# Gate logits and the turn of x1 into user-major rows: two TensorE products against one of 136 columns

## The chip, the cores and the metric

The kernel runs on one core of one Trainium2 chip. The metric is the device time of one execution in microseconds (us). The kernel before has been run three times: the median is 1422.55 us (1422.31 to 1427.97).

## What is computed

The reference is a graph layer followed by a mixture of eight experts, for 10000 users of 128 features. Cut to what matters:

```python
h = item_feat @ W_item.T + b_item
x1 = x + relu(adj @ h + layernorm(x) @ W_user.T + b_user)      # adj is 10000 x 10000, float32
t = layernorm(x1)
logits = t @ gate_w + gate_b                                   # eight experts
idx = argmax(softmax(logits)); prb = the largest probability
pos = the user's place among those of its expert; kept = pos < 1563
y = relu(t @ w1[idx] + b1[idx]) @ w2[idx] + b2[idx]            # 128 -> 512 -> 128
out = x1 + nan_to_num(y * prb * kept)
```

## The kernel before, in words

**Work and stages.** The users are cut into 20 blocks of 500 (four tiles of 125, `TILES`, `TP`). For each block the product with the 400 MB matrix `adj` runs over the 10000 items in 20 groups `g` of four chunks of 128 items (the last group has three). Each number of `adj` and of `h` is split into a high and a low part, and three products (high x high, high x low, low x high) of 500 columns each go into one PSUM bank, `acc[q]`, with `q` the block's parity. The result is feature-major: features on partitions, users along the columns.

**Who does what in a group.** SyncE (SP, L372) loads the group into a ring of ten buffers; ScalarE (ACT, L483) makes the high part into a ring of four; VectorE (DVE, L672) makes the low part; TensorE (PE) does eight products from the high part (L1077, L1079) and, one group later, four from the low part (L1088). Semaphores `hi_used` and `lo_used` give the buffers back.

**What follows a block.** The order is written out by hand in the `body` of each engine. In block `b` each engine, between two groups, also does a piece of the blocks `b-1` and `b-2`:
- ACT takes the accumulator of block `b-1` through relu into `gnn` (`take_gnn`, L493, group 4); DVE adds x to it (`add_x`, L709, group 5). `gnn` is then x1, feature-major.
- PE, behind the low part in group 5, runs `logits(b-1)` (L1120): four products with a tile of `gnn` as the stationary side and the 8 columns of the centred gate weights as the moving side, into bank 4. Then `turn_x1(b-1)` (L1129): four transposes of the same four tiles through the identity, into bank 2.
- ACT copies the turned rows into the record buffer `rec` (`take_x1`, L502, group 10). DVE takes their mean and variance (`x1_variance`), GpSimd (POOL) the reciprocal root (`x1_scale`, L973), and one block later DVE scales the logits and picks the expert (`choose`, from L728, group 2, and `pick`, group 3), PE counts (`count`, group 4), DVE sets the slots (`assign`, `settle`), and POOL scatters the records (L981) and the rows of the output (L987) with indirect DMAs.

**The last block** (`is_last`) does this earlier: `add_x(18)` in group 4, PE's logits and turn in group 2, ACT's copy in group 6. POOL then clears unused slots of the records (`set_zeros`, `clear_slots`, `clear_edges`, L994 to L1012), which waits for `x1_scale(18)` in its own queue and for PE's group 3, and scatters the blocks 17, 18 and 19.

**The end.** After the loop come 32 units of 392 slots for the experts. The first two are begun inside the last block. Between them lie `logits(19)`, `turn_x1(19)`, and on DVE `choose(19)` to `settle(19)`; PE's in-order queue has `count(19)` in the midst of the units' products.

The lines of the gate and the turn on PE, which the prediction is about:

```python
for j in range(TILES):
    last = nc.tensor.matmul(to[:, j, :], gnn[:, j * TP:(j + 1) * TP], const("gate_w"),
                            start=True, stop=True)
```

```python
for j in range(TILES):
    last = nc.tensor.transpose(turned[0:TP, j * HID:(j + 1) * HID], gnn[:, j * TP:(j + 1) * TP],
                               ident)
```

Of the kernel before, what the change touches and what calls it, by code (L numbers as in the profile page):

```python
# [5 lines left out]
ALU = mybir.AluOpType  # L6
# [6 lines left out]
HID = 128  # L13
# [4 lines left out]
TILES = 4  # L18
TP = 125
# [19 lines left out]
EXPERTS = 8  # L39
# [30 lines left out]
_at = 0  # L70
for _name, _n in (("ident", 128), ("tri", TP), ("rev", TILES * EXPERTS), ("tok", 2 * TILES),
                  ("w_user", HID), ("gate_w", EXPERTS), ("gate_b", TILES * EXPERTS),
                  ("run_at", 1), ("run_no", EXPERTS), ("edge_of", EXPERTS),
                  ("starts", RUNS), ("edge_no", 1), ("edge_at", 1), ("b_user", 1),
                  ("expert_no", EXPERTS), ("unit_end", BODY)):
    COLS[_name] = (_at, _at + _n)
    _at += _n
# [3 lines left out]
def build(nc, adj_m, adj_r, items_t, x, x_t, consts, item_consts, w1, w2, rec_d, out):  # L81
    ctx = ExitStack()
    with ctx:
# [12 lines left out]

        ident = const("ident")
        h_hi = sb("h_hi", [128, CHUNKS * HID], F32R)
        h_at = nc.sbuf_base
# [81 lines left out]
        def in_h_lo(at, n):  # L181
# [15 lines left out]
        acc = bank[0:2]  # L197
        ps_gnn, ps_x, _, ps_h0, ps_h1 = bank[2:7]
        ps_logit, ps_logit_last = (t[0:TP, 2 * EXPERTS:(2 + TILES) * EXPERTS].rearrange("p (j e) -> p j e", j=TILES)
                                   for t in (bank[4], bank[7]))  # L200
        ps_count = bank[7][0:TP, 0:EXPERTS]
# [45 lines left out]
        norm_ready = sem("norm_ready")  # L247
        logits_done = sem("logits_done")
        shifted = sem("shifted")
# [202 lines left out]
        def _(act):  # L452
# [35 lines left out]
            def take_gnn(n, q):  # L488
                act.wait_ge(lo_used, (n + 1) * GROUPS)
                if not isinstance(n, int) or n > 0:  # L490
                    act.wait_ge(logits_done, n)
                    act.wait_ge(x1_turned, n)
                nc.scalar.activation(gnn[:, 0:BLOCK], acc[q][:, 0:BLOCK], ACT.Relu,  # L493
                                     bias=const("b_user")).then_inc(gnn_ready, 1)

            def take_x1(n, q, pairs):
                act.wait_ge(x1_turned, n + 1)
                if not isinstance(n, int) or n > 1:
                    act.wait_ge(scattered[q], pairs * (TILES * 16))
                    act.wait_ge(passed_on[q], pairs * (TILES * 16))  # L500
                turned = ps_out if is_last(n) else ps_gnn
                nc.scalar.copy(rec[:, q, :, 0:HID],  # L502
                               turned[0:TP, :].rearrange("p (j d) -> p j d", j=TILES)).then_inc(x1_ready, 1)

# [129 lines left out]
        def _(dve):  # L634
            v = nc.vector
            chain = Chain(dve, dve_chain, 22)
            x_chain = Chain(dve, x_chain_done, 2)
# [84 lines left out]
            def choose(n, q):  # L722

                chain.round(n)
                dve.wait_ge(logits_done, n + 1)
                dve.wait_ge(rstd_ready, n + 1)
                raw_logit = ps_logit_last if is_last(n) else ps_logit
                chain.link(v.tensor_tensor(lg[:, :, :], raw_logit, rec[:, q, :, C_RSTD:C_RSTD + 1].broadcast_to(  # L728
                    [TP, TILES, EXPERTS]), ALU.mult))
                chain.link(v.tensor_tensor(lg[:, :, :], lg[:, :, :], gate_b, ALU.add))  # L730
                chain.did(v.tensor_scalar(tok[:, :, :], tok[:, :, :], float(BLOCK), None, ALU.add))
                chain.link(v.tensor_reduce(mx[:, :], lg[:, :, :], AX.X, ALU.max))
                v.tensor_tensor(lgm[:, :, :], lg[:, :, :], each(mx), ALU.subtract).then_inc(shifted, 1)
# [318 lines left out]
        def _(pe):  # L1052
# [60 lines left out]

            def logits(n):
                pe.wait_ge(x1T_ready, n + 1)
                if not isinstance(n, int) or n > 0:
                    pe.wait_ge(shifted, n)
                to = ps_logit_last if is_last(n) else ps_logit
                for j in range(TILES):
                    last = nc.tensor.matmul(to[:, j, :], gnn[:, j * TP:(j + 1) * TP], const("gate_w"),  # L1120
                                            start=True, stop=True)
                last.then_inc(logits_done, 1)

            def turn_x1(n):
                if not isinstance(n, int) or n > 0:
                    pe.wait_ge(x1_ready, n)
                turned = ps_out if is_last(n) else ps_gnn
                for j in range(TILES):
                    last = nc.tensor.transpose(turned[0:TP, j * HID:(j + 1) * HID], gnn[:, j * TP:(j + 1) * TP],  # L1129
                                               ident)  # L1130
                last.then_inc(x1_turned, 1)
# [13 lines left out]
            def body(i, q):  # L1145
                b = i * 2 + q
                fixed = isinstance(b, int)
                for g in range(GROUPS):
# [11 lines left out]
                    if g == (2 if is_last(b) else 5) and (not fixed or b > 0):  # L1160
                        logits(b - 1)
                        turn_x1(b - 1)
# [67 lines left out]
            mid(0, 0, range(3, FC))  # L1230
            logits(BLOCKS - 1)
            turn_x1(BLOCKS - 1)
# [85 lines left out]
```

## Time and profile before

| | value |
|---|---|
| three runs | 1427.97, 1422.31, 1422.55 us, median 1422.55 |
| the profiled execution | 1432.02 us, its span 1429.9 us |
| PE busy | 1364.4 us of the span (95%), 6200 instructions |
| DVE, ACT, POOL busy | 1183.2 (83%), 955.3 (67%), 570.8 us (40%) |
| mean granted TensorE clock | 0.977 of full speed |
| HBM read and written | 427.92 and 23.50 MB |

The span is the time from the first to the last instruction. Matmul and weight-load records are separate: PE is the product, PEld the loading of its stationary side, and the two overlap. Every product of two plain float32 operands shows as two PE records and two PEld records (80 products of the gate are 160 records); a transpose, or a product of the rounded parts (`fp32r`), shows as one. Matmul records overlap one another, so the price of one in a stream is read from the distance of the starts, not from its length.

### The profile page before, as it was taken

To read this page: it belongs to the slowest core of one execution; us is meant where nothing else is said; L and a number is where in the kernel's file an instruction comes from. 1 tells how busy PE (TensorE), PEld (TensorE's weight loads), DVE (VectorE), ACT (ScalarE), POOL (GpSimd) and SP (SyncE) were. 2 spreads that over 40 slices of the span, in tenths; PEclk is the share of its full clock that TensorE was granted. 3 is DMA by queue.
4 is the path that set the end of the run, shared out by engine and by line. 5 is a ranking of instruction groups with operands and counts; after the bars stand their busy time and mean duration, and the time that the engine had idled before them with its cause. 6 is when DMAs were issued, how large, how long until landed. Compare 5 with 4: busy or idle time off the path is not lost. (4 is left out here: it accounts for less than half of the span.)

```text
span 1429.9 us, 20127 instructions
## 1 busy us (share of the span) xinstructions
PE 1364.4 (95%) x6200; PEld 1108.9 (78%) x6200; DVE 1183.2 (83%) x1747; ACT 955.3 (67%) x930; POOL 570.8 (40%) x359
## 2 busy tenths in 40 slices
PE   8999999999999999999999999999999997888983
PEld 6888888888888888888888888888888776666662
DVE  6999989889889899898898998988988955756664
ACT  5776776767667667767676677676766656665661
POOL 0001236145163262350541623614416556556555
PEclk9999999999999999999999999999999999899987
DMA  9999999999999999999999999999999852222210
GB/s 335 359 393 408 406 388 363 379 373 358 371 367 364 366 372 374 358 370 376 366 367 366 370 364 371 366 375 364 366 369 373 301 172 71 69 71 59 60 33 3
DMA packets 92140, 440.99 MB, mean 308 GB/s; under 512 B 22610, under 2 KB 27873, under 8 KB 92098
## 3 DMA queue, kind: packets, MB, share of 16 engines
q1 hardware_dynamic: 68505, 417.98, 78.0%
q0 software_dynamic: 17632, 12.24, 3.1%
q10 hardware_dynamic: 5960, 10.24, 2.2%
q8 instruction: 21, 0.34, 0.1%
q14 instruction: 22, 0.17, 0.0%
HBM read 427.92 MB, written 23.50 MB: 316 GB/s over the span
## 5 line engine op out<-in xcount | busy, mean ns | idle before, releaser
L672 DVE TENSOR_TENSOR a_lo<-raw,a_hi 128x2000 fp32r<-128x2000 f32 (+1 forms) x400 | 869.1, 2189 | 109.2 <-ACT a_hi L483 103.1
L483 ACT CAST a_hi<-raw 128x2000 fp32r<-128x2000 f32 (+1 forms) x400 | 724.4, 1825 | 296.2 <-PE bank L1079 183.9
L1077 PE MATMUL bank<-a_hi,h_hi 128*128 128x500 f32 x1560 | 623.7, 400 | 0.0
L1079 PE MATMUL bank<-a_hi,h_lo 128*128 128x500 f32 x1560 | 606.8, 389 | 0.0
L1088 PE MATMUL bank<-a_lo,h_hi 128*128 128x500 f32 x1560 | 418.5, 389 | 0.0
L1077 PEld LDWEIGHTS bank<-a_hi,h_hi 128*128 128x128 f32 x1560 | 294.0, 188 | 66.0 <-issue 9.4
L1079 PEld LDWEIGHTS bank<-a_hi,h_lo 128*128 128x128 f32 x1560 | 294.6, 189 | 59.9 <-issue 4.4
L1088 PEld LDWEIGHTS bank<-a_lo,h_hi 128*128 128x128 f32 x1560 | 293.5, 188 | 59.4
L973 POOL TENSOR_TENSOR late<-ve,neghalf 125x4 f32<-125x4 f32 x20 | 55.3, 2765 | 596.2 <-DVE ve L689 596.1
L981 POOL DMA_INDIRECT records<-late,slot x80 | 174.6, 2183 | 22.9 <-issue 22.9
L1045 POOL DMA_INDIRECT out<-raw x128 | 130.1, 1016 | 106.4 <-DVE raw L936 70.1
L987 POOL DMA_INDIRECT out<-late,kept_out x76 | 133.1, 1751 | 23.1 <-issue 23.1
L1203 PE MATMUL bank<-raw 128*128 128x392 f32 x256 | 96.8, 522 | 0.8 <-ACT raw L601 0.8
L593 ACT ACTIVATE raw<-bank,raw 128x392 f32<-128x392 f32 x128 | 66.8, 587 | 28.2 <-PE bank L1194 18.1
L919 DVE TENSOR_TENSOR raw<-bank,raw 98x512 f32<-98x512 f32 x32 | 22.0, 687 | 68.1 <-remote 50.5
L1203 PEld LDWEIGHTS bank<-raw 128*128 128x128 f32 x256 | 50.1, 207 | 31.3 <-issue 7.0
L1192 PE MATMUL bank<-h_lo 128*128 128x392 f32 x128 | 51.6, 403 | 18.5 <-issue 10.1
L969 POOL TENSOR_TENSOR xrs<-xve,neghalf 125x4 f32<-125x4 f32 x20 | 30.4, 1522 | 91.9 <-DVE xve L689 91.5
L601 ACT ACTIVATE raw<-bank,raw 128x392 f32<-128x392 f32 x32 | 18.9, 590 | 51.7 <-remote 24.1
L575 ACT ACTIVATE raw<-raw 98x128 f32<-98x128 f32 x128 | 52.8, 491 | 0.9 <-DMA raw<-records 0.9
L1193 PE MATMUL bank<-h_lo 128*128 128x392 f32 x128 | 47.1, 368 | 0.0
L1194 PE MATMUL bank<-h_lo 128*128 128x392 f32 x128 | 47.0, 367 | 0.0
(126 smaller groups left out, 873.0 us busy)
## 6 DMA issues: line engine op xcount, KB each, us to landing
raw<-adj_m SPq DMA_DIRECT2D x380, 1000.0 KB, 6.1
raw<-adj_m SPq DMA_DIRECT2D x20, 500.0 KB
raw<-records SPq DMA_DIRECT2D x32, 202.1 KB
xT<-x_t ACTq DMA_DIRECT2D x20, 250.0 KB
late<-items_t SPq DMA_DIRECT2D x19, 256.0 KB, 4.7
xb<-x ACTq DMA_DIRECT2D x20, 224.0 KB
raw<-w SPq DMA_DIRECT2D x8, 258.5 KB
raw<-w SPq DMA_DIRECT2D x8, 256.0 KB
```

The lines of the kernel that those rows point to most:

```text
L483: last = nc.scalar.copy(a_hi[:, g % HI_RING, 0:m], raw[:, g % RAW, 0:m])
L575: last = nc.scalar.activation(x2q[:, k % 2, j, :], recq[:, k, j, 0:HID], ACT.Identity, scale=recq[:, k, j, C_RSTD:C_RSTD + 1], bias=recq[: ...
L593: nc.scalar.activation(hm[:, k % 2, f, :], ps_mid[f][:, 0:UNIT], ACT.Relu, bias=bias_of(k, f)).then_inc(hm_ready, 1)
L672: last = v.tensor_tensor(a_lo[:, g % RAW, 0:m], raw[:, g % RAW, 0:m], a_hi[:, g % HI_RING, 0:m].bitcast(F32), ALU.subtract)
L973: p.tensor_tensor(rec[:, q, :, C_RSTD:C_RSTD + 1], ve[:, :].unsqueeze(2), neghalf[:, :].unsqueeze(2), ALU.pow).then_inc(rstd_ready, 1)
L981: p.indirect_dma_start(rec_d, bass.IndirectOffsetOnAxis(ap=slot[:, q, j:j + 1], axis=0), rec[:, q, j, :], None, bounds_check=SLOTS - 1, oo ...
L987: p.indirect_dma_start(out, bass.IndirectOffsetOnAxis(ap=kept_out[:, q, j:j + 1], axis=0), rec[:, q, j, 0:HID], None, bounds_check=USERS - ...
L1045: p.indirect_dma_start(out, bass.IndirectOffsetOnAxis(ap=recq[:, n % BODY, j, C_TOK:C_TOK + 1].bitcast(U32), axis=0), yout[:, n % YRING, j ...
L1077: nc.tensor.matmul(acc[q][:, 0:BLOCK], h_hi[:, k * HID:(k + 1) * HID], a, start=(k == 0), stop=False)
L1079: last = nc.tensor.matmul(acc[q][:, 0:BLOCK], h_lo[:, k * HID:(k + 1) * HID], a, start=False, stop=False)
L1088: last = nc.tensor.matmul(acc[q][:, 0:BLOCK], h_hi[:, k * HID:(k + 1) * HID], a_lo[:, g % RAW, c * BLOCK:(c + 1) * BLOCK], start=False, st ...
L1203: last = nc.tensor.matmul(ps_y[:, 0:UNIT], wb2[:, w, f * HID:(f + 1) * HID], hm[:, k % 2, f, :], start=(f == 0), stop=(f == FC - 1))
```

## The change

One product takes the place of two. The 128 columns of the identity and the 8 columns of the centred gate weights now stand side by side in the constants, and `turn_w` is the view over both. `turn_x1` does four plain float32 products with a tile of `gnn` as the stationary side and these 136 columns as the moving side. The four outputs of 136 columns don't fit one bank, so two go to bank 2 and two to bank 4 (for the last block: 6 and 7). ACT's copy into `rec` becomes two copies of two tiles each; DVE's first operation of `choose` becomes two, one for each bank. The semaphore `logits_done` goes: `choose` waits for `x1_ready` in its place, and the product waits for both `x1_ready` and `shifted` of the block before, which the two older steps did apiece.

```diff
-for _name, _n in (("ident", 128), ("tri", TP), ("rev", TILES * EXPERTS), ("tok", 2 * TILES),
-                  ("w_user", HID), ("gate_w", EXPERTS), ("gate_b", TILES * EXPERTS),
+for _name, _n in (("ident", HID), ("gate_w", EXPERTS), ("tri", TP), ("rev", TILES * EXPERTS), ("tok", 2 * TILES),
+                  ("w_user", HID), ("gate_b", TILES * EXPERTS),
...
+        turn_w = cst[:, COLS["ident"][0]:COLS["gate_w"][1]]
...
-        ps_gnn, ps_x, _, ps_h0, ps_h1 = bank[2:7]
-        ps_logit, ps_logit_last = (t[0:TP, 2 * EXPERTS:(2 + TILES) * EXPERTS].rearrange("p (j e) -> p j e", j=TILES)
-                                   for t in (bank[4], bank[7]))
+        _, ps_x, _, ps_h0, ps_h1 = bank[2:7]
+        TURN = HID + EXPERTS
+        ps_turn, ps_turn_last = ([t[0:TP, a:a + 2 * TURN].rearrange("p (j c) -> p j c", j=2) for t, a in pair]
+                                 for pair in (((bank[2], 0), (bank[4], 0)),
+                                              ((bank[6], 0), (bank[7], 2 * EXPERTS))))
...
                 act.wait_ge(lo_used, (n + 1) * GROUPS)
                 if not isinstance(n, int) or n > 0:
-                    act.wait_ge(logits_done, n)
                     act.wait_ge(x1_turned, n)
...
-                turned = ps_out if is_last(n) else ps_gnn
-                nc.scalar.copy(rec[:, q, :, 0:HID],
-                               turned[0:TP, :].rearrange("p (j d) -> p j d", j=TILES)).then_inc(x1_ready, 1)
+                for half, turned in enumerate(ps_turn_last if is_last(n) else ps_turn):
+                    last = nc.scalar.copy(rec[:, q, 2 * half:2 * half + 2, 0:HID], turned[:, :, 0:HID])
+                last.then_inc(x1_ready, 1)
...
-            chain = Chain(dve, dve_chain, 22)
+            chain = Chain(dve, dve_chain, 23)
...
-                dve.wait_ge(logits_done, n + 1)
+                dve.wait_ge(x1_ready, n + 1)
                 dve.wait_ge(rstd_ready, n + 1)
-                raw_logit = ps_logit_last if is_last(n) else ps_logit
-                chain.link(v.tensor_tensor(lg[:, :, :], raw_logit, rec[:, q, :, C_RSTD:C_RSTD + 1].broadcast_to(
-                    [TP, TILES, EXPERTS]), ALU.mult))
+                for half, turned in enumerate(ps_turn_last if is_last(n) else ps_turn):
+                    pair = slice(2 * half, 2 * half + 2)
+                    chain.link(v.tensor_tensor(lg[:, pair, :], turned[:, :, HID:TURN],
+                                               rec[:, q, pair, C_RSTD:C_RSTD + 1].broadcast_to([TP, 2, EXPERTS]),
+                                               ALU.mult))
...
-            def logits(n):
+            def turn_x1(n):
                 pe.wait_ge(x1T_ready, n + 1)
                 if not isinstance(n, int) or n > 0:
+                    pe.wait_ge(x1_ready, n)
                     pe.wait_ge(shifted, n)
-                to = ps_logit_last if is_last(n) else ps_logit
+                turned = ps_turn_last if is_last(n) else ps_turn
                 for j in range(TILES):
-                    last = nc.tensor.matmul(to[:, j, :], gnn[:, j * TP:(j + 1) * TP], const("gate_w"),
+                    last = nc.tensor.matmul(turned[j // 2][:, j % 2, :], gnn[:, j * TP:(j + 1) * TP], turn_w[:, :],
                                             start=True, stop=True)
-                last.then_inc(logits_done, 1)
-
-            def turn_x1(n):
-                if not isinstance(n, int) or n > 0:
-                    pe.wait_ge(x1_ready, n)
-                turned = ps_out if is_last(n) else ps_gnn
-                for j in range(TILES):
-                    last = nc.tensor.transpose(turned[0:TP, j * HID:(j + 1) * HID], gnn[:, j * TP:(j + 1) * TP],
-                                               ident)
                 last.then_inc(x1_turned, 1)
...
-                        logits(b - 1)
                         turn_x1(b - 1)
...
-            logits(BLOCKS - 1)
             turn_x1(BLOCKS - 1)
```

PE's order around the turn in block 1, before (L1077 and L1079 are the high part's products, L1088 the low part's; `bank` is any PSUM bank):

```order
L1079 MATMUL bank<-a_hi,h_lo 128x500
L1088 MATMUL bank<-a_lo,h_hi 128x500 x4
L1120 MATMUL bank<-cst,gnn 125x8 x4
L1129 MATMUL bank<-cst,gnn 125x128 x4
L1077 MATMUL bank<-a_hi,h_hi 128x500
```

and in the changed kernel, where the same lines are numbered L1082, L1091 and L1080:

```order
L1082 MATMUL bank<-a_hi,h_lo 128x500
L1091 MATMUL bank<-a_lo,h_hi 128x500 x4
L1124 MATMUL bank<-cst,gnn 125x136 x4
L1080 MATMUL bank<-a_hi,h_hi 128x500
```

Eight products became four, at the same place of the queue; in the other blocks it is the same, in the last block behind group 2.

DVE's order in `choose`, before:

```order
L672 TENSOR_TENSOR a_lo<-raw,a_hi 128x2000
L728 TENSOR_TENSOR lg<-bank,late 125x32
L730 TENSOR_TENSOR lg<-lg,cst 125x32
L731 TENSOR_SCALAR tok<-tok 125x8
```

and in the changed kernel:

```order
L673 TENSOR_TENSOR a_lo<-raw,a_hi 128x2000
L730 TENSOR_TENSOR lg<-bank,late 125x16 x2
L733 TENSOR_TENSOR lg<-lg,cst 125x32
L734 TENSOR_SCALAR tok<-tok 125x8
```

One operation became two of half the size, and nothing else moved on DVE.

## Rows read from the trace of the kernel before

**Rows 1.** The page, part 1: busy us (share of the span) xinstructions.

```profile
span 1429.9 us, 20127 instructions
PE 1364.4 (95%) x6200; PEld 1108.9 (78%) x6200; DVE 1183.2 (83%) x1747; ACT 955.3 (67%) x930; POOL 570.8 (40%) x359
```

**Rows 2.** Busy time by stretch; last three numbers: granted PE clock, DMA share, GB/s.

```profile
80.00:1105.00 1025.00, 1025.00 (x4652) 843.47 (x4651) 913.81 (x1233) 719.58 (x526) 388.15 (x190) 1.00 0.99 372
...
1171.00:1430.00 259.00, 203.16 (x886) 150.86 (x885) 151.49 (x329) 142.90 (x315) 147.15 (x144) 0.88 0.20 53
```

**Rows 3.** Waits, whole span, SyncE: engine line waited for: us, times, longest.

```profile
SPq L372 <- PE bank L1088: 814.1, 354, 9.6
```

**Rows 4.** Waits of all engines from 80 to 1110 us: us in total, times, longest.

```profile
ACT a_hi L483 <- PE bank L1079: 174.7, 191, 2.2
DVE a_lo L672 <- ACT a_hi L483: 99.0, 129, 2.4
```

**Rows 5.** PE in order of time, block 10's turn: start us, length us, line.

```profile
610.05 0.94 PE L1120 MATMUL bank<-cst,gnn 128*125 128x8 f32 x8
610.84 0.68 PE L1129 MATMUL bank<-cst,gnn 128*125 128x128 f32 x4
611.27 0.47 PE L1077 MATMUL bank<-a_hi,h_hi 128*128 128x500 f32 x1
611.58 0.39 PE L1079 MATMUL bank<-a_hi,h_lo 128*128 128x500 f32 x1
611.81 0.39 PE L1077 MATMUL bank<-a_hi,h_hi 128*128 128x500 f32 x1
```

**Rows 6.** PE in block 0: four plain float32 products of 128 columns (x8).

```profile
41.76 1.05 PE L1060 MATMUL bank<-gnn,late 128*128 128x128 f32 x8
42.57 0.47 PE L1077 MATMUL bank<-a_hi,h_hi 128*128 128x500 f32 x1
42.88 0.39 PE L1079 MATMUL bank<-a_hi,h_lo 128*128 128x500 f32 x1
```

**Rows 7.** PE in block 10: one plain float32 product of 500 columns (x2).

```profile
636.23 1.00 PE L1111 MATMUL bank<-colsT,cst 128*128 128x500 f32 x2
...
637.30 0.39 PE L1079 MATMUL bank<-a_hi,h_lo 128*128 128x500 f32 x1
```

**Rows 8.** The last block's turn, in order of time; [idle before <-releaser].

```profile
1114.39 1.85 PE L1120 MATMUL bank<-cst,gnn 128*125 128x8 f32 x8 [2.65 <-DVE gnn L709]
...
1117.50 0.62 PE L1079 MATMUL bank<-a_hi,h_lo 128*128 128x500 f32 x1
1117.92 0.62 PE L1077 MATMUL bank<-a_hi,h_hi 128*128 128x500 f32 x1
...
1117.32 0.59 ACT L502 COPY late<-bank 125x512 f32<-125x512 f32 x1 [1.84 <-PE bank L1129]
...
1120.13 1.02 POOL L973 TENSOR_TENSOR late<-ve,neghalf 125x4 f32<-125x4 f32 x1 [19.65 <-DVE ve L689]
```

**Rows 9.** Busy time by stretch, last block, columns as in rows 2.

```profile
1118.00:1119.00 1.00, 1.00 (x4) 0.83 (x3) 1.00 (x4) 0.00 (x0) 0.00 (x0) 0.50 0.00 0
```

**Rows 10.** Groups on DVE and ACT: busy us, mean ns | idle before, releaser.

```profile
L728 DVE TENSOR_TENSOR lg<-bank,late 125x32 f32<-125x32 f32 x20 | 3.7, 183 | 0.0
...
L469 ACT CAST h_hi<-h_raw 128x512 fp32r<-128x512 f32 x19 | 11.7, 617 | 8.1 <-DVE h_raw L650 8.0
...
L469 ACT CAST h_hi<-h_raw 128x256 fp32r<-128x256 f32 x1 | 0.4, 396 | 0.0
```

**Rows 11.** After the loop: POOL, then PE, in order of time.

```profile
1177.11 1.19 POOL L981 DMA_INDIRECT records<-late,slot  x1 [0.30 <-issue]
1178.32 1.06 POOL L973 TENSOR_TENSOR late<-ve,neghalf 125x4 f32<-125x4 f32 x1
...
1181.89 0.38 PE L1136 MATMUL bank<-run,cst 125*125 125x8 f32 x2 [3.10 <-DVE run L745]
```

**Rows 12.** Busy time by stretch, block 1, columns as in rows 2.

```profile
80.00:137.00 57.00, 57.00 (x258) 46.83 (x257) 53.42 (x51) 44.14 (x32) 7.96 (x3) 1.00 1.00 400
```

More of the change, by code:

```diff
@@ L247, in build @@
         norm_ready = sem("norm_ready")
-        logits_done = sem("logits_done")
         shifted = sem("shifted")
```

## The prediction

> **What bounds the kernel now.** I read the busy shares first: PE 95%, DVE 83%, ACT 67% of the span [rows 1]. A share over a whole span mixes stages, so the table by stretch comes next: from 80 to 1105 us, the blocks 1 to 18 nearly, PE is busy for 1025.00 of 1025 us at clock 1.00, while DVE has 914 and ACT 720 us [rows 2]. A busy PE need not be the one that sets the pace, since its records overlap. So the waits decide: ACT waits for PE to give back the high ring (174.7 us), DVE waits for ACT (99.0 us) [rows 4], and SyncE's loads wait for PE's low products for 814.1 us [rows 3]. PE itself has no wait in that stretch. All others follow PE, so what is taken out of PE's stream there comes off the time, one for one. One doubt stays: the DMA engines show a share of 0.99 at 372 GB/s [rows 2].
>
> The last block is another case. PE stands 2.65 us for `add_x(18)`, and the turn behind it runs at half clock [rows 8], as does the stretch after it, with 0.50 granted at 1118 us [rows 9]; what PE did before was idling. POOL's long chain of clearing and scattering starts when `x1_scale(18)` comes, for which it had waited 19.65 us [rows 8], and after the loop it is still at it: at 1178.32 `x1_scale(19)` runs right behind a scatter, with no idle time, and PE's count waits 3.10 us for what follows [rows 11]. From the last block on, the end hangs on POOL's chain and then on the units.
>
> **PE's two steps against one, per block.** The price is the distance of starts over the group and the product behind it, because the first large product after a short one is late as well (0.31 in place of 0.23 us). Before: from L1120's first start at 610.05 to L1079's at 611.58 is 1.53 us; a large product in the stream takes 0.23 (611.81 less 611.58); so the turn costs **1.30 us** for 12 passes, 8 of 8 columns and 4 of 128 [rows 5]. An 8-column pass costs nearly what a 128-column one does, 0.099 to 0.107 us, so the gate's 8 columns pay for their stationary side, not for their columns.
>
> After: four float32 products of 136 columns are 8 passes. The nearest row is L1060 in block 0: four float32 products of 128 columns with 128 weight columns, from 41.76 to 42.88, less 0.23, are 0.89 us [rows 6]. The eight columns more come from a long product: two passes of 500 columns take 637.30 less 636.23 less 0.23, that is 0.84 us [rows 7], or 0.84 ns a column and pass; 8 passes x 8 columns x 0.84 ns is 0.05 us. New price **0.94 us**, gain 0.36 us a block. Bounds: if the columns hid wholly behind the weights, 8 passes at the 0.10 of L1120's would be 0.79 us, a gain of 0.5; on the other side the rows show a plain product of 128 columns as 8 passes where the turn had 4, and I take as the far end that the group costs what the old one did, a gain of nothing. I take 0.36, since L1060 is this very shape but for 8 columns.
>
> The Trainium skill, "TensorE: Matmul & The Clock Gate", section "Terms", speaks against the change: a transpose mode makes float32 transposes four times faster, and the change leaves that mode. By that rule the sum would be the third rival's below. This case's rows show a factor of two: L1060 has two passes for each product, L1129 one, and a pass has the same price [rows 5, 6].
>
> **Blocks 1 to 18** hold the turns of users' blocks 0 to 17: 18 x 0.36 = **6.5 us**.
>
> **The last block's turn** (block 18) runs at half clock: from 1114.39 to L1079's start at 1117.50 is 3.11 us, less one large product at half clock, 0.42 (1117.92 less 1117.50), leaves 2.69 [rows 8]. Twice 0.94 is 1.89: 0.80 gained. The stall before it stays, because it hangs on DVE's and ACT's chain behind PE's own last products of block 18; the extra DVE operation in `choose(17)` lies ahead of a low part that waits for ACT, and is covered by such waits [rows 4]. Behind the turn ACT's copy is on the chain to POOL: one copy becomes two. From casts of 512 and 256 columns, 617 and 396 ns [rows 10], two halves cost 0.18 us more than the whole. So POOL starts **0.6 us** earlier still.
>
> **What is added elsewhere.** ACT pays 0.18 us more a block, hidden in 174.7 us of waiting for PE over 18 blocks; if that cover were gone, 0.18 us a block would come back as 3 us. DVE pays one small operation more, 183 ns [rows 10] and some 40 for the link, hidden by 99 us of waiting [rows 4]; uncovered it would be 4 us. `choose` now waits for `x1_ready`, but it already waits for the root that comes after it, so nothing new ends there. PE's added wait in front of the gate product was in front of the turn before. No DMA is added or moved, and SP's and POOL's queues have the same instructions.
>
> **After the loop** `turn_x1(19)` is not on the chain: POOL is not free before 1178.30 [rows 11]. The second operation of `choose(19)` is on it, ahead of PE's count: **0.2 us** more.
>
> **Sum.** 6.5 + 0.6 - 0.2 = 6.9 us less. The profiled execution took 1432.02 us for a span of 1429.9, and would take 1425.1. It was 9.5 us slower than the median of the three runs, and the stretch after the loop, with a mean clock of 0.88 [rows 2], is where an execution can differ from another; the turns in the loop don't depend on it. Against the median: 1422.55 - 6.9 = **1415.7 us**.
>
> **The rivals.**
> 1. *The DMA engines pace the loop.* If PE's stream is stretched to fit the loads, a shorter stream only waits. For it: the share of 0.99. The Trainium skill, "Perfetto Trace Analysis", section "Roofline", gives 358 GB/s as a core's share and some 120% of it as what one core alone can reach. Against it: in block 1 the same queues moved 400 GB/s [rows 12], 372 is wanted and 375 would be after the change, and the loads wait for PE for 814 us [rows 3]. It gives no gain, about 1422.5. The same time comes if the new passes cost what the old twelve did. Chance 0.12.
> 2. *The tail moves by itself.* The stretch behind the loop has idle spots at which the clock falls; shifted and shortened steps may move a cold stretch. The runs before differ by 5.7 us and the profiled one by 9.5. With the loop's gain this gives about 1410 or about 1421. Chance 0.15, 0.08 of it below and 0.07 above.
> 3. *Slower: the plain product costs four transposes.* The four transposes advance in 0.43 us (611.27 less 610.84) [rows 5]; four times that, times 136/128, is 1.83 us against 1.30 for old gate and turn together: 0.53 us lost in each of 18 blocks and 1.1 in the last, 10.6 us, giving 1433. It decides from the point where a pass of the new product takes more than 1.30/8 = 0.16 us. Against it: L1060's passes took 0.11 [rows 6], and PE shows no hint of another price for `gnn` as the stationary side. Chance 0.05, with all else that ends slower.
>
> That the change doesn't do what it says can be left aside: the order shows four products of 136 columns where eight stood.
>
> **Numbers.** My forecast, 1415.7 with some 1.5 us to either side, has 0.68. About 0.5% (7.1 us) is what a measurement of this kernel can tell from no change, so the line is at 1415.4, and my forecast lies on it: half of its 0.68 falls below. Faster: 0.34 + 0.08 = 0.42. Same: 0.34 + 0.12 + 0.07 = 0.53. Slower: 0.05. The range goes from 1411.5, which takes in the bound of 0.5 us a block (18 x 0.14 = 2.5 us more gain) and part of the low tail, to 1423.0, which takes in the case of no gain; outside are the slower rival and the rest of the low tail.
>
> **What would show it.** The distance from the new product's first start to the second large product's start, less 0.23, should be 0.94 us; 1.3 or more speaks for the third rival. The distance between two blocks should fall by 0.36 us; if the turn is short and this doesn't fall, something else paces, and PE would show new idle time before L1080 with a DMA or ACT as its releaser. In the last block POOL's first root should come 0.6 us earlier against PE's group 0. The share of the stretch behind the loop should be as before within 0.3 us, unless its clock has moved; if more than 2 us come from there, the forecast's sum is wrong even where its total is right.

## The result and the profile after

The changed kernel takes **1418.74 us** (median of 20 runs, 1407.83 to 1426.03), the kernel before, run beside it, 1426.03 us (20 runs, 1417.32 to 1432.04). The ratio is 0.9943, 95% interval 0.9922 to 0.9963: 8.1 us less, between 5.3 and 11.1 (the two medians alone lie 7.3 us apart; differences in us that are given with an interval are worked out from the ratio). The forecast was 6.9 us less and 1415.7 us; before itself came out 3.5 us above the three runs on which that total stood. On two later occasions, where before takes 1388 us, the ratio was 0.9962 (0.9947 to 0.9977) and 0.9960 (0.9946 to 0.9973), that is 5.3 and 5.6 us.

The profiled execution of the changed kernel took 1418.38 us. The head of its page, against [rows 1]:

```profile
span 1416.3 us, 20014 instructions
...
PE 1349.2 (95%) x6120; PEld 1096.6 (77%) x6120; DVE 1183.4 (84%) x1767; ACT 955.2 (67%) x950; POOL 562.6 (40%) x359
```

PE has 80 records fewer: 240 of the gate and the turn became 160. DVE and ACT have 20 more each.

PE in order of time around block 10's turn, the view of [rows 5]:

```profile
607.57 1.09 PE L1124 MATMUL bank<-cst,gnn 128*125 128x136 f32 x8
608.41 0.47 PE L1080 MATMUL bank<-a_hi,h_hi 128*128 128x500 f32 x1
608.72 0.39 PE L1082 MATMUL bank<-a_hi,h_lo 128*128 128x500 f32 x1
```

From 607.57 to 608.72 is 1.15 us; less 0.23 it is 0.92, where [rows 5] gave 1.30. The busy time by stretch and the waits from 80 to 1110 us, as in [rows 2, 4]:

```profile
80.00:1105.00 1025.00, 1024.65 (x4608) 841.80 (x4607) 918.90 (x1261) 725.67 (x548) 382.29 (x190) 1.00 0.99 375
```

```profile
ACT a_hi L485 <- PE bank L1082: 171.5, 191, 1.8
DVE a_lo L673 <- ACT a_hi L485: 91.2, 110, 2.2
```

PE is still busy throughout at the full clock. ACT's cover went from 174.7 to 171.5 us and DVE's from 99.0 to 91.2: the added operations were paid out of waiting (e2 tries this apart). The loads rose from 372 to 375 GB/s. The DMA engines followed.

The last block, against [rows 8]; the turn waits as before, and then come ACT's copies, DVE's queue and POOL's root:

```profile
1108.26 2.18 PE L1124 MATMUL bank<-cst,gnn 128*125 128x136 f32 x8 [2.65 <-DVE gnn L710]
1110.08 0.78 PE L1080 MATMUL bank<-a_hi,h_hi 128*128 128x500 f32 x1
1110.66 0.62 PE L1082 MATMUL bank<-a_hi,h_lo 128*128 128x500 f32 x1
```

```profile
1110.48 0.65 ACT L503 COPY late<-bank 125x256 f32<-125x256 f32 x2 [1.11 <-PE bank L1124]
```

```profile
1108.13 4.38 DVE L673 TENSOR_TENSOR a_lo<-raw,a_hi 128x2000 fp32r<-128x2000 f32 x2
1112.43 0.86 DVE L684 BATCH_NORM_STATS2 st<-late 125x6 f32<-125x128 f32 x4
```

```profile
1113.99 1.02 POOL L976 TENSOR_TENSOR late<-ve,neghalf 125x4 f32<-125x4 f32 x1 [19.62 <-DVE ve L690]
```

The turn's group takes 2.40 us where it took 3.11, and ACT has its rows at 1111.1. But DVE comes to them at 1112.43 only, behind two low parts. From the turn's start to POOL's root it is 5.73 us, and it was 5.74 before. Here the forecast had 0.6 us.

The length of this one turn hangs on the clock as well, and the clock differs from execution to execution. PE stands 2.65 us in front of it each time, but the granted clock over the group was 0.50 in these two profiles, and 1.00 in e5, the changed kernel again:

```profile
1109.85 1.19 PE L1124 MATMUL bank<-cst,gnn 128*125 128x136 f32 x8 [2.65 <-DVE gnn L710]
1110.79 0.48 PE L1080 MATMUL bank<-a_hi,h_hi 128*128 128x500 f32 x1
1111.11 0.38 PE L1082 MATMUL bank<-a_hi,h_lo 128*128 128x500 f32 x1
```

There the group took 1.26 us. In the pair e12 (before) and e9 (changed) it took 2.60 and 2.27 us, at clocks of 0.61 and 0.53. So the 0.71 us gained here belong to one pair of executions.

After the loop, against [rows 11], POOL and then DVE's first operations of `choose(19)`:

```profile
1169.01 1.19 POOL L984 DMA_INDIRECT records<-late,slot  x1 [0.30 <-issue]
1170.23 1.05 POOL L976 TENSOR_TENSOR late<-ve,neghalf 125x4 f32<-125x4 f32 x1
```

```profile
1171.39 0.38 DVE L730 TENSOR_TENSOR lg<-bank,late 125x16 f32<-125x16 f32 x2
1171.81 0.19 DVE L733 TENSOR_TENSOR lg<-lg,cst 125x32 f32<-125x32 f32 x1
```

The root follows a scatter without idle time again, and the two halves take 0.42 us up to the next operation.

Where executions differ is best seen in a table of stretches, made from the starts of a few instructions in each profile: the first turn, the last block's turn, POOL's roots of blocks 18 and 19, PE's count of block 19, and the end of the span.

| profile | first turn at | first to last turn | to root 18 | to root 19 | to count 19 | to the end |
|---|---|---|---|---|---|---|
| before | 100.36 | 1014.03 | 5.74 | 58.19 | 3.57 | 248.0 |
| changed | 101.55 | 1006.71 | 5.73 | 56.24 | 3.69 | 242.4 |

The two spans differ by 13.6 us, and only 7.3 of it lies in the loop, where all the turns but two are. Of the rest, 5.6 us lie behind the last count and 2.0 between the two roots, and 1.2 were lost ahead of the first turn. These stretches scatter in the profiles of the experiments too: behind the last count before, the change and e1 to e4 have 240.9 to 248.0 us.

### The profile page after: what moved, and what is told of

Its sections match the earlier page's. It is cut to its first block and busy times, and to the rows that moved or that the text cites. A ratio compares the mean times of both kernels' runs of the same rounds, so it can differ in the third digit from the quotient of the medians.

```text
span 1416.3 us, 20014 instructions
## 1 busy us (share of the span) xinstructions
PE 1349.2 (95%) x6120; PEld 1096.6 (77%) x6120; DVE 1183.4 (84%) x1767; ACT 955.2 (67%) x950; POOL 562.6 (40%) x359
## 5 line engine op out<-in xcount | busy, mean ns | idle before, releaser
L1080 PE MATMUL bank<-a_hi,h_hi 128*128 128x500 f32 x1560 | 623.4, 400 | 0.0
L1082 PE MATMUL bank<-a_hi,h_lo 128*128 128x500 f32 x1560 | 606.2, 389 | 0.0
L1091 PE MATMUL bank<-a_lo,h_hi 128*128 128x500 f32 x1560 | 418.6, 389 | 0.0
L1080 PEld LDWEIGHTS bank<-a_hi,h_hi 128*128 128x128 f32 x1560 | 294.0, 188 | 65.9 <-issue 9.5
L1082 PEld LDWEIGHTS bank<-a_hi,h_lo 128*128 128x128 f32 x1560 | 294.3, 189 | 59.6 <-issue 4.4
L1091 PEld LDWEIGHTS bank<-a_lo,h_hi 128*128 128x128 f32 x1560 | 293.4, 188 | 59.1
L984 POOL DMA_INDIRECT records<-late,slot x80 | 170.3, 2128 | 22.9 <-issue 22.9
L922 DVE TENSOR_TENSOR raw<-bank,raw 98x512 f32<-98x512 f32 x32 | 22.0, 688 | 58.4 <-remote 47.3
L1186 PE MATMUL bank<-h_lo 128*128 128x392 f32 x128 | 50.0, 390 | 11.5 <-ACT raw L594 8.9
L1188 PE MATMUL bank<-h_lo 128*128 128x392 f32 x128 | 46.2, 361 | 0.0
L1187 PE MATMUL bank<-h_lo 128*128 128x392 f32 x128 | 46.0, 360 | 0.0
```

Of the source, the lines that this page charges most:

```text
L984: p.indirect_dma_start(rec_d, bass.IndirectOffsetOnAxis(ap=slot[:, q, j:j + 1], axis=0), rec[:, q, j, :], None, bounds_check=SLOTS - 1, oo ...
L1080: nc.tensor.matmul(acc[q][:, 0:BLOCK], h_hi[:, k * HID:(k + 1) * HID], a, start=(k == 0), stop=False)
L1082: last = nc.tensor.matmul(acc[q][:, 0:BLOCK], h_lo[:, k * HID:(k + 1) * HID], a, start=False, stop=False)
L1091: last = nc.tensor.matmul(acc[q][:, 0:BLOCK], h_hi[:, k * HID:(k + 1) * HID], a_lo[:, g % RAW, c * BLOCK:(c + 1) * BLOCK], start=False, st ...
L1186: nc.tensor.matmul(to, w1_hi[:, w, cols], x2q_hi[:, k % 2, :], start=True, stop=False)
```

## The experiments

All comparisons with before are ratios with their 95% intervals. Runs e1 to e4 ran together on one chip, and so did e5 to e8 and e9 to e12; before took 1426.91, 1388.69 and 1387.79 us in them, so only ratios and stretches are compared across the sets. The interval of a ratio can be too narrow: e12 is the kernel before against itself and came out at 1.0012 (1.0003 to 1.0021), 2 us apart. "The loop" is the way from the first turn's start to the last block's turn's start, 18 blocks.

**e1: the gate products twice.**

```diff
-                for j in range(TILES):
+                for j in [*range(TILES), *range(TILES)]:
                     last = nc.tensor.matmul(to[:, j, :], gnn[:, j * TP:(j + 1) * TP], const("gate_w"),
```

> The kernel before with the four gate products issued twice (8 passes of 8 columns more in each block). Theory PE (the loop is PE's stream, one for one): the group grows from 1.30 to about 2.1 us (8 x 0.10), the way from the first turn's start to the last block's turn start grows from 1014.0 by 18 x 0.8 = 14 us, and the time by 15 to 17 us (about 1.1%). Rival (something else paces and the change's gain came from the tail or from chance): the group grows but the block distance grows by less than half of it, and the time by under 7 us.

Measured: 1.0100 (1.0051 to 1.0150), about 14 us slower (7 to 21), a little under the 15 to 17 expected. PE around the turn:

```profile
617.59 1.81 PE L1120 MATMUL bank<-cst,gnn 128*125 128x8 f32 x16
619.25 0.68 PE L1129 MATMUL bank<-cst,gnn 128*125 128x128 f32 x4
...
620.00 0.39 PE L1079 MATMUL bank<-a_hi,h_lo 128*128 128x500 f32 x1
```

The group grew from 1.53 to 2.41 us, 0.88 for eight passes, 0.11 each. The loop took 1029.75 us, 15.7 more than before's 1014.03, and 18 x 0.88 is 15.8. The loop is PE's stream, one for one; the rival falls.

**e2: the new layout with the old steps on PE.** The edit is one against the changed kernel:

```diff
+                    nc.tensor.matmul(turned[j // 2][:, j % 2, HID:TURN], gnn[:, j * TP:(j + 1) * TP], const("gate_w"),
+                                     start=True, stop=True)
...
+            def turn_x1(n):
+                turned = ps_turn_last if is_last(n) else ps_turn
+                for j in range(TILES):
+                    last = nc.tensor.transpose(turned[j // 2][:, j % 2, 0:HID], gnn[:, j * TP:(j + 1) * TP], ident)
```

> The changed kernel's two banks, ACT's two copies, DVE's two operations and the new wait, but PE's old steps (gate products of 8 columns, transposes of 128). Theory: all of that is covered, so the time is that of the kernel before, up to 0.3 us slower; the group on PE stays 1.30 us and the loop 1014 us. Rival (a cover is gone): 3 us slower for ACT's copies, 4 for DVE's operation, or both. Rival (part of the measured gain came from the other layout): faster than before by 1 us or more in the loop.

Measured: 1.0003 (0.9974 to 1.0032), which by itself leaves 4 us to either side; the loop is the sharper measure. The group stays at 1.53 to 1.54 us, less 0.23. ACT's second copy, DVE's second operation and the new waits cost nothing that shows: the covers hold. The loop is 1013.57 us and not 1014.03. The 0.46 us are small but they repeat (below, at e4).

**e3: the turn as a plain product, the gate as it was.**

```diff
-                    last = nc.tensor.transpose(turned[0:TP, j * HID:(j + 1) * HID], gnn[:, j * TP:(j + 1) * TP],
-                                               ident)
+                    last = nc.tensor.matmul(turned[0:TP, j * HID:(j + 1) * HID], gnn[:, j * TP:(j + 1) * TP],
+                                            ident, start=True, stop=True)
```

> The kernel before with the turn as four plain float32 products by the identity in place of four transposes; gate products untouched. It prices leaving the transpose mode alone. Reading of the rows (a plain product has two passes of the transposes' price): the group grows by 4 x 0.107 = 0.43 us, the loop by 7.7 us, the time by about 8 us. By the rule that the transpose mode is four times faster: by 1.3 us a block, 23 us in the loop.

Measured: 1.0069 (1.0041 to 1.0096), about 10 us slower.

```profile
614.53 0.94 PE L1120 MATMUL bank<-cst,gnn 128*125 128x8 f32 x8
615.32 1.12 PE L1129 MATMUL bank<-cst,gnn 128*125 128x128 f32 x8
616.19 0.47 PE L1077 MATMUL bank<-a_hi,h_hi 128*128 128x500 f32 x1
616.50 0.39 PE L1079 MATMUL bank<-a_hi,h_lo 128*128 128x500 f32 x1
```

Four products are eight passes and take 0.87 us (615.32 to 616.19) where four transposes took 0.43: a factor of two, and the loop is 7.9 us longer (1021.95), 18 x 0.44. The rule of four from the Trainium skill, "TensorE: Matmul & The Clock Gate", section "Terms", doesn't hold for this shape. A pass has the same price in both modes; the transpose has half as many.

**e4: gate products of 128 columns.** The order of the constants is the changed kernel's here too, so that the 8 gate columns stand behind the identity.

```diff
+        gate_wide = cst[:, COLS["gate_w"][1] - 128:COLS["gate_w"][1]]
+        ps_wide = bank[4][0:TP, :].rearrange("p (j c) -> p j c", j=TILES)
...
+                    if not is_last(n):
+                        last = nc.tensor.matmul(ps_wide[:, j, :], gnn[:, j * TP:(j + 1) * TP], gate_wide,
+                                                start=True, stop=True)
```

> The kernel before with the gate products taking 128 columns (120 of the identity and the 8 of the gate) in place of 8, into the whole of bank 4; the last block's kept at 8. Theory (a short pass pays for its stationary side, so columns up to some 125 are free): 8 x 8 passes of 128 columns cost as the 8-column ones do, the group stays within 0.05 us of 1.30 and the loop within 1 us of 1014. Rival (columns are paid on top): 120 columns x 0.84 ns x 8 passes = 0.8 us a block, 14 us in the loop.

Measured: 0.9979 (0.9949 to 1.0009).

```profile
610.41 1.03 PE L1123 MATMUL bank<-cst,gnn 128*125 128x128 f32 x8
...
611.63 0.47 PE L1079 MATMUL bank<-a_hi,h_hi 128*128 128x500 f32 x1
611.94 0.39 PE L1081 MATMUL bank<-a_hi,h_lo 128*128 128x500 f32 x1
```

From 610.41 to 611.94 is 1.53 us, as with 8 columns. So 120 columns more in each of eight passes are free. This is the reason of the change's gain: the identity's columns ride in passes that the gate had paid for already, the four transposes' 0.43 us go, and only the eight columns on top, above 128, are paid for, 0.05 us, which leaves 0.38.

Why the 8-column pass costs that much isn't shown. That it waits for its stationary side to be loaded is the theory that the run was built on, but no run changed the stationary side. A row of the kernel before says that 128 stationary columns alone don't cost it: four transposes behind the loop, each with 128 stationary columns over 98 partitions and 98 moving columns, at a clock of 1.00.

```profile
1257.79 0.50 PE L1179 MATMUL bank<-cst,raw 98*128 98x98 f32 x4
1258.12 0.44 PE L1192 MATMUL bank<-h_lo 128*128 128x392 f32 x1
```

They advance by 0.08 us each, less than the 0.11 of a gate pass with 125 stationary and 8 moving columns. Whether the fewer partitions or the transpose mode make the difference was not tried.

The loop is 1013.57 us again, as in e2. What these two share with the changed kernel, and before, e1 and e3 don't, is the order of the constants. Two starts of each, `w_user`'s product and the next count, first of the kernel before, then of e2:

```profile
183.17 1.00 PE L1111 MATMUL bank<-colsT,cst 128*128 128x500 f32 x2
...
210.45 0.28 PE L1136 MATMUL bank<-run,cst 125*125 125x8 f32 x2
```

```profile
183.52 1.00 PE L1114 MATMUL bank<-colsT,cst 128*128 128x500 f32 x2
...
210.77 0.28 PE L1136 MATMUL bank<-run,cst 125*125 125x8 f32 x2
```

27.28 against 27.25 us: 0.03 us a block, in the same stretch of the loop's blocks each time. It goes with the layout, which is what e2, e4 and the changed kernel share; `w_user`'s weights, at the head of the stretch, now stand eight columns further on. The product itself is no shorter by more than 0.01 us (1.07 and 1.06 to the second large product behind it); the 0.03 gather over the large products of the next 6 us. Why wasn't tried.

**e5: the changed kernel again.**

> The changed kernel once more, for a second profile beside e6 to e8. Theory: the group 1.15 - 0.23 = 0.92 us again, the way from the first turn to the last block's turn 1006.7 again within 0.3 us, and the time about 0.5% below before. The time from the count of block 19 to the end, which was 248.0 before and 242.4 in the first profile of the change, should differ again, to either side, if it is chance.

Measured: 0.9962 (0.9947 to 0.9977). Group 1.15 less 0.23, loop 1006.72 us, both as before. But the first turn was at 103.13 us, and the end came 202.6 us after the count, not 242.4. That is the 40 us between the sets; in e12 before has 204.5. It need not be the chip: by the record, e1 to e4 (before 1426.91 us) and e9 to e12 (1387.79 us) ran on the chip with the same number. In the profiles of before, of the change and of e1 to e4, ACT and DVE have waits behind the loop that the profile can't put down to an instruction ("remote"); the waits of the changed kernel's first profile from 1175 us to the end:

```profile
DVE raw L922 <- remote: 47.3, 10, 7.4
...
ACT raw L602 <- remote: 38.2, 10, 4.9
```

In e5 and in all profiles after it there are no such rows. What these waits are stays open.

**e8: the new product twice.**

```diff
-                for j in range(TILES):
+                for j in [*range(TILES), *range(TILES)]:
                     last = nc.tensor.matmul(turned[j // 2][:, j % 2, :], gnn[:, j * TP:(j + 1) * TP], turn_w[:, :],
```

> The changed kernel with the product of 136 columns issued twice. Theory PE: 8 passes more at 0.113 us, 0.91 us a block, 16.3 us in the loop, 1.8 us in the last block at half clock that do not reach POOL's root unless the turn then ends behind DVE's low parts (which it does by then: from 1108.3 on, 4.2 us, DVE comes at 1112.4, so 0 to 0.5 us), in all 16 to 17 us slower than the changed kernel. Rival: under half of that.

Measured: 1397.96 us against e5's 1382.74, 15.2 us more, a little under the 16 to 17 expected (to before 1.0074, 1.0059 to 1.0088).

```profile
617.17 2.02 PE L1124 MATMUL bank<-cst,gnn 128*125 128x136 f32 x16
...
619.25 0.39 PE L1082 MATMUL bank<-a_hi,h_lo 128*128 128x500 f32 x1
```

The group is 2.08 us, 0.93 for eight passes more, 0.116 each; the loop 1023.40, so 16.7 more, 18 x 0.93. POOL's root still starts 5.73 us after the turn. That alone says little, because this execution's last turn ran at full clock, and its 16 passes took 1.95 us, where the eight at half clock in the change's first profile took 1.98. All profiles together say it: with the turn in its old place ACT has its rows between 1.88 us (e5) and 3.68 us (e1) after the turn's start, DVE comes to them at 4.16 or 4.17, and the root follows at 5.73 or 5.74. So DVE's queue holds it.

**e6 and e7: the last block.** e6 puts the last turn one group later, where `add_x` is just done; e7 moves ACT's copy and DVE's variance one group earlier as well.

```diff
-                    if g == (2 if is_last(b) else 5) and (not fixed or b > 0):
+                    if g == (3 if is_last(b) else 5) and (not fixed or b > 0):
```

```diff
-                    if g == 6 and is_last(b):
+                    if g == 5 and is_last(b):
                         take_x1(b - 1, 0, i + q - 1)
...
-                        if g == 6:
+                        if g == 5:
                             x1_variance(b - 1, 0)
+                        if g == 6:
                             find_edges()
```

> The changed kernel with the last block's turn behind PE's group 3 in place of group 2. PE's 2.65 us of standing and the half clock behind it go, so PE is some 5 us earlier at the end of the loop. Theory (from there the end hangs on POOL, whose root waits for DVE's own queue of low parts and not for the turn): the root of block 18 starts 5.7 us after the old turn's place as before, within 0.3, and the time is that of the changed kernel within 1 us. Rival (PE's stall sets the end): 3 to 5 us faster.

> e6 with ACT's copy and DVE's variance of block 18 one group earlier too (5 in place of 6). Theory (DVE's queue is what holds POOL's root): the root starts 2.2 us earlier, by one low part, against the end of block 18, and the time is 2 us below the changed kernel. Rival (the turn holds it): no more than e6 gives. If POOL's chain isn't what the end hangs on, no gain in either.

Measured: e6 0.9926 (0.9911 to 0.9941), 1377.06 us against e5's 1382.74; e7 0.9937 (0.9924 to 0.9950), 1379.15 us. So the rival's size in e6, though the profile shows the root 5.73 us after the turn, where the theory has it. In e7 the root is 2.15 us earlier, as expected, and the time no better than e6's. Both were repeated beside the changed kernel.

**e9, e10, e11, e12: the changed kernel, e6, e7 and before once more.**

> The changed kernel, beside e10 and e11 on one chip, to settle what they are worth. The loop 1006.7 us again; its time some 6 to 7 us below before.

> e6 again. In e6 the median was 5.7 us under the changed kernel's, where its profile showed only 1.5 us after the loop (POOL's way from the root of block 18 to that of block 19) and 2.1 us in block 0, where the kernels don't differ. Theory A (POOL's chain sets the end, the start was chance): 1 to 2 us faster than the changed kernel. Theory B (PE's earlier end of the loop, 2.65 us of standing and the half clock behind it, counts in full): 4 to 6 us again.

> e7 again. POOL's root is 2.1 us earlier against the turn, as in e7; if its chain gives that back in the indirect DMAs, as e7's profile showed (the way from root to root 56.9 us in place of 54 to 56), the time is e10's within 1 us; if e7's long chain was chance, it is 2 us under e10's.

> The kernel before, for a profile on the same chip as e9. Theory: first turn to the last block's turn 1013.6 to 1014.0 us, so 6.9 to 7.3 more than e9; the stretch from count 19 to the end the same as e9's within 2 us (or, on a chip where executions scatter by 10 us, within 6). Rival (the change also shortens the stretch behind the loop): e9's is shorter by 3 us or more on every chip.

Measured, as ratio to before: e9 0.9960 (0.9946 to 0.9973), e10 0.9930 (0.9917 to 0.9943), e11 0.9931 (0.9918 to 0.9943), e12 1.0012 (1.0003 to 1.0021). In medians 1381.66, 1377.65, 1378.37 and 1389.75 us. The stretches:

| profile | first turn at | first to last turn | to root 18 | to root 19 | to count 19 | to the end |
|---|---|---|---|---|---|---|
| e5 (changed) | 103.13 | 1006.72 | 5.74 | 55.81 | 3.69 | 202.6 |
| e6 | 101.06 | 1006.73 | 5.73 | 54.27 | 3.72 | 202.6 |
| e7 | 101.57 | 1006.72 | 3.58 | 56.92 | 3.69 | 202.2 |
| e12 (before) | 101.34 | 1014.03 | 5.73 | 56.81 | 3.59 | 204.5 |
| e9 (changed) | 102.12 | 1006.73 | 5.73 | 56.91 | 3.69 | 203.3 |
| e10 (as e6) | 101.65 | 1006.72 | 5.73 | 54.30 | 3.69 | 203.0 |
| e11 (as e7) | 102.02 | 1006.72 | 3.59 | 57.01 | 3.68 | 206.2 |

e12 against e9 is the change on one chip: 7.3 us in the loop and 1.2 behind the last count; 0.8 lost ahead of the first turn, 0.1 between the roots and 0.1 at the count. The 0.8, and 1.2 in the first pair, lie ahead of all that the change touches on PE; e2, with the new layout, has its first turn at 100.73, and eight profiles of the changed kernel and its variants scatter from 101.06 to 103.13. Whether some of it belongs to the change isn't settled; if it does, 6.0 to 6.4 us are left of the 7.2. The rival of a shorter tail (3 us or more on every chip) falls: it is 1.2 us here.

e10 is 4.0 us under e9 in the median, e6 was 5.7 under e5: theory B's size, and the path is another than either theory had. POOL's clearing in e9 and in e10, from the root over the last clearing DMA to its landing:

```profile
1114.58 1.02 POOL L976 TENSOR_TENSOR late<-ve,neghalf 125x4 f32<-125x4 f32 x1 [19.63 <-DVE ve L690]
...
1135.83 2.37 POOL L1007 DMA_INDIRECT records<-h_raw,clear_edge  x1 [0.30 <-issue]
...
1152.02 1.14 POOL L350 TENSOR_TENSOR carrier_pool<-ones 125x1 f32<-125x1 f32 x1 [13.82 <-DMA records<-h_raw,clear_edge]
```

```profile
1114.10 1.02 POOL L976 TENSOR_TENSOR late<-ve,neghalf 125x4 f32<-125x4 f32 x1 [19.63 <-DVE ve L690]
...
1134.57 2.36 POOL L1007 DMA_INDIRECT records<-h_raw,clear_edge  x1 [0.30 <-issue]
...
1148.23 1.80 POOL L350 TENSOR_TENSOR carrier_pool<-ones 125x1 f32<-125x1 f32 x1 [11.30 <-DMA records<-h_raw,clear_edge]
```

The landing is waited for 11.30 us in place of 13.82. In all ten profiles with the turn in its old place this wait is 13.17 to 13.82 us, in e6 it is 11.13. And the busy time by stretch in e9, whose last two numbers are the DMA engines' share and GB/s, then in e10:

```profile
1108.00:1120.00 12.00, 11.15 (x48) 9.62 (x49) 11.68 (x25) 7.02 (x11) 4.23 (x5) 0.86 0.57 209
...
1130.00:1140.00 10.00, 10.00 (x48) 8.38 (x47) 9.06 (x20) 7.43 (x5) 7.28 (x4) 1.00 1.02 412
```

```profile
1108.00:1120.00 12.00, 12.00 (x59) 9.95 (x59) 11.68 (x24) 9.51 (x11) 4.70 (x5) 1.00 0.98 355
...
1130.00:1140.00 10.00, 10.00 (x46) 8.31 (x45) 9.62 (x27) 6.95 (x4) 6.02 (x4) 1.00 0.89 327
```

While PE stands for `add_x(18)` it gives no buffers back, and the loads of the last `adj` groups fall to 209 GB/s. They are caught up at 412 GB/s while the clearing DMAs are being issued. In the wait itself, from 1138.20 to 1152.02 in e9 and from 1136.93 to 1148.23 in e10, the queues move less in both, and again less in e10:

```profile
1138.20:1152.02 13.82, 13.82 (x61) 11.19 (x60) 11.80 (x17) 7.41 (x6) 0.00 (x1) 1.00 0.59 229
```

```profile
1136.93:1148.23 11.30, 11.30 (x50) 9.08 (x49) 11.06 (x16) 6.18 (x5) 0.00 (x1) 1.00 0.42 170
```

The reading is that the loads which were held back come in the clearing's way. It was made from the profiles, and no run tried it apart. The other profiles bear it out: over the 14 us from 3 us ahead of the last turn's start, the less the queues moved, the longer, by and large, the way from root to root (e7 and e11, whose chain starts earlier against the turn, are left out).

| GB/s over these 14 us | profiles | root to root, us |
|---|---|---|
| 194, 202 | before, e2 | 58.2, 58.4 |
| 215 to 244 | e1, e12, e4, e9, changed | 56.2 to 56.9 |
| 270 to 283 | e3, e8, e5 | 55.2 to 55.8 |
| 342, 353 | e6, e10 | 54.3, 54.3 |

In the third line PE stood as long as in the first two, but its last turn ran at full clock. So the half clock behind the standing seems to have a part in it too.

PE's own lead is given back before the loop ends. In e10 it waits again for DVE at the count and for ACT at the slots' turn, where e9 has no such waits:

```profile
1127.96 0.38 PE L1131 MATMUL bank<-run,cst 125*125 125x8 f32 x2 [1.24 <-DVE run L748]
...
1155.63 0.56 PE L1173 MATMUL bank<-cst,raw 98*128 98x98 f32 x4 [1.72 <-ACT raw L576]
```

The last product of the loop starts 50.79 us after the last turn in e10 and 51.62 in e9 (e6 50.69, e5 50.49). So "PE is some 5 us earlier at the end of the loop", as e6's expectation had it, didn't come true.

The two profiled pairs differ by 3.4 us (e9, e10) and 3.6 us (e5, e6). Of this 2.6 and 1.5 lie from root to root, and 0.5 and 2.1 ahead of the first turn, where the kernels don't differ. The medians differ by 4.0 and 5.7 us, and what they have above the 2.6 and 1.5 isn't located.

e11's root is 2.1 us earlier, as expected, and the way from root to root is 2.7 us longer (57.01 against 54.30), as in e7 (56.92 against 54.27): given back in POOL's own DMAs, twice. It is no better than e10. **The edit of e6 and e10 beats both kernels**: 0.9926 and 0.9930 of before, where the change has 0.9962 and 0.9960 beside them, with intervals that don't meet.

## Why the prediction was right, and where it was not

- **What bounds the loop**: right. Doubling the gate (e1) and doubling the new product (e8) each came back in the loop one for one, 15.7 for 15.8 us and 16.7 for 16.7. The rival with the DMA engines falls, since the loads followed both ways (375 GB/s in the changed kernel, 372 before, 367 in e1, from 80 to 1105 us).
- **The new group**: forecast 0.94 us, measured 0.92; gain 0.38 a block in place of 0.36. The two rows used, four products of 128 columns and a column's price from a long one, were enough. Its reason, that the 8 columns pay for their stationary side, stays a reading (e4 shows the columns free, and no run changed the stationary side). 18 x 0.38 is 6.9 us.
- **What the forecast didn't have**: 0.03 us a block, 0.46 in all, from the new order of the constants (e2, e4). With it the loop's gain is 7.3 us, forecast 6.5.
- **The last block's turn**: the group gained 0.71 us in the first pair, forecast 0.80. That it runs at half clock held for that pair only (0.3 us gained in e12 and e9, and full clock in e5). The step that failed is the next one, "So POOL starts 0.6 us earlier still": it gained 0.0. The forecast followed the chain over ACT's copy and left out DVE's own queue; the variance stands behind two low parts, which end 1.3 us after ACT's rows are there. The spread of ACT's copies over all profiles (1.88 to 3.68 us after the turn's start, the root unmoved) and e7 and e11, where the variance was moved and the root came 2.15 us earlier, show it from both sides. The added price of ACT's second copy was too high as well: 0.07 us (0.58 to 0.65), not 0.18.
- **The covers** on ACT and DVE: right, by e2's loop, which didn't grow; by e2's time within its interval.
- **After the loop**: `choose(19)` costs 0.20 us more up to the next operation, as forecast; at the count 0.10 to 0.12 are left.
- **Sum**: forecast 6.9 us less; by the stretches 7.3 - 0.1 = 7.2; measured 8.1 (5.3 to 11.1) in one set and 5.3 and 5.6 in two others. The stretches' 7.2 lies within all three intervals (in the last two, 3.2 to 7.4 and 3.7 to 7.5 us), near the upper end of two. That the sum came so close is in part luck: the 0.6 us for POOL never came, and 0.4 from cheaper passes and 0.46 from the layout, which it didn't have, stood in for them.
- **The rivals**: that four transposes' price is paid for a product is refuted by e3. The tail that moves by itself is real, 5.6 us between the two profiles first compared, but it isn't the change's: before and changed agree within 1.2 us in e12 and e9. By the prediction's own sign (more than 2 us from behind the loop make the sum wrong even where the total is right) the first pair, with 7.5 us from there, would have spoken against it; this second pair, with 1.1, doesn't. That the line at 0.5% would run through the forecast was so; the ratio was 0.57% below before on the first occasion and 0.38 and 0.40% on the two others.

## What to carry to other kernels

Price a short float32 matmul by the pass, not by its columns: with 125 stationary columns a pass took about 0.11 us for 8 moving columns and for 128 alike, and 0.116 for 136. So products that share a stationary tile are worth putting side by side, and up to that width the added moving columns cost nothing. A step that is made shorter on one engine gives its time to the next only if that engine is not behind its own queue. And look at what an engine's standing stops: here the way from root to root was the longer the more the loads had been held back. That is a reading of twelve profiles and no experiment on the loads alone.

## What the runs showed of the hardware that was not expected

- A constant's place can matter a little: the stretch that begins with `w_user`'s product took 27.25 us in place of 27.28 with the new order of the constants, in the loop's blocks of every kernel that had it. The cause is open.
- The same program takes 1427 us on one occasion and 1388 on another, with equal loops (1014.03 us in both profiles of before) and 248.0 against 204.5 us from the last count to the end.
- After the same 2.65 us of standing, the same turn had a granted clock of 0.50, 0.53 or 1.00 in three executions of the changed kernel, and took 2.40, 2.27 or 1.26 us.
- The last of nine indirect DMAs that clear records was waited for 13.2 to 13.8 us in ten profiles, and 11.1 and 11.3 us in the two where the loads had not been held up before.
